# The place of the mixing matmuls in a step of the first scan: behind the first stream's convolution, or behind the second's

## What is computed

```python
x = x + _L0_conv_ref(_gn(x), centers, spreads, bias)   # token mixing, 4 heads
x = x + _L1_conv_ref(_gn(x), W)                        # a scan over the 64 rows

# _L0: einsum('mns,bwnvs->bwmvs', posmap, xr), posmap a softmax of 128x128 for each of 4 heads, plus a bias
# _L1, every image by itself:
def step(carry, row):
    new = row + relu(conv1d_same(carry, W))            # 9 taps over the tokens, 64 -> 64 channels
    return (new, new)
```

## Time and profile before

| what | value |
|---|---|
| median of 3 runs | 891.21 us (890.06 to 892.18) |
| the profiled execution | 893.26 us |
| its span | 891.3 us |
| busy in the span | PE 86%, PEld 81%, DVE 67%, ACT 53%, POOL 48% |
| granted TensorE clock, mean | 0.966 |
| first scan, first convolution of step 1 to last output transpose | 199.68 to 615.35 us |
| second scan, from its step 1 | 625.46 to 891 us |

### The profile page before, as it was taken

How to read it: one execution, slowest core, us unless ns; L and a number is a source line. 1 busy time by engine, 2 the same in 40 slices (tenths; PEclk the granted TensorE clock), 3 DMA queues, 4 the chain that set the end, 5 groups by cost and what they waited for, 6 DMA issues and landing times.

```text
span 891.3 us, 17386 instructions
## 1 busy us (share of the span) xinstructions
PE 764.4 (86%) x5546; PEld 718.1 (81%) x5546; DVE 595.3 (67%) x1265; ACT 476.8 (53%) x918; POOL 431.1 (48%) x416
## 2 busy tenths in 40 slices
PE   1677777769889898988989898997999999999997
PEld 1555556558888788887988887887999999999997
DVE  6699999955657567575776757555555555555553
ACT  1255555565456455555555555456555555555552
POOL 1677777725446445554454555453333333333332
PEclk9999998889999999999999999999899999999999
DMA  9755454023243243343333331111223222232323
GB/s 189 140 110 117 99 116 95 16 57 83 60 95 84 60 89 88 67 90 84 71 82 87 84 71 43 38 41 42 49 61 68 62 65 65 62 68 59 71 59 71
DMA packets 203149, 68.11 MB, mean 76 GB/s; under 512 B 137556, under 2 KB 203092, under 8 KB 203092
## 3 DMA queue, kind: packets, MB, share of 16 engines
q1 hardware_dynamic: 203092, 67.43, 34.8%
HBM read 33.85 MB, written 33.55 MB: 76 GB/s over the span
## 4 chain that ended last, share of the span: by engine, by line
PE 60%; DVE 17%; POOL 13%; issue 6%; ACT 2%; DVEq 0%; POOLq 0%; ACTq 0%
PE ps_conv L976 29%; PE ps_conv L980 14%; POOL xs L352 11%; PE ps_mix L892 9%; PE ps_out L968 4%; DVE st L668 3%; DVE st L550 3%; DVE carry L758 2%; DVE dev L613 2%; POOL total L379 2%; PE ps_in L905 2%; PE ps_small L882 1%; ACT x_paired L438 1%; DVE dev L618 1%; DVE x_sb L661 1%
## 5 line engine op out<-in xcount | busy, mean ns | idle before, releaser
L379 POOL TENSOR_TENSOR total<-x_paired,carry 128x256 f32<-128x256 f32 x256 | 188.3, 736 | 366.4 <-DVE carry L758 347.7
L480 ACT ACTIVATE carry_h<-carry 128x256 fp32r<-128x256 f32 x252 | 105.6, 419 | 298.3 <-DVE carry L758 298.3
L766 DVE TENSOR_TENSOR carry_l<-carry,carry_h 128x256 fp32r<-128x256 f32 x252 | 174.0, 690 | 90.6 <-ACT carry_h L480 90.6
L976 PE MATMUL ps_conv<-carry_h,wh 128*128 128x256 f32 x1280 | 221.7, 304 | 4.3 <-ACT carry_h L480 4.3
L758 DVE SCALAR_TENSOR_TENSOR carry<-ps_conv,rows 128x256 f32<-128x256 f32 x256 | 108.1, 422 | 163.4 <-PE ps_conv L980 158.5
L352 POOL TENSOR_TENSOR xs<-x_sb,rstd 128x512 f32<-128x512 f32 x104 | 193.5, 1886 | 39.5 <-DVE rstd L643 33.7
L438 ACT ACTIVATE x_paired<-ps_in,shift 64x512 f32<-64x512 f32 (+1 forms) x256 | 174.5, 682 | 68.4 <-PE ps_in L905 65.0
L976 PE MATMUL ps_conv<-carry_h,wl 128*128 128x256 f32 x1280 | 199.0, 286 | 0.0
L980 PE MATMUL ps_conv<-carry_l,wh 128*128 128x256 f32 x1280 | 198.9, 287 | 0.0
L976 PEld LDWEIGHTS ps_conv<-carry_h,wh 128*128 128x128 f32 x1280 | 180.2, 192 | 8.2 <-ACT carry_h L480 4.8
L976 PEld LDWEIGHTS ps_conv<-carry_h,wl 128*128 128x128 f32 x1280 | 175.0, 192 | 0.0
(11 more groups left out here) (92 smaller groups left out, 406.1 us busy)
## 6 DMA issues: line engine op xcount, KB each, us to landing
out_dram<-staged SPq DMA_DIRECT2D x256, 128.0 KB, 2.4
x_sb<-in_x_dram SPq DMA_DIRECT2D x52, 512.0 KB, 4.1
rows<-in_x_dram SPq DMA_DIRECT2D x12, 512.0 KB, 4.0
x_paired<-in_L_conv_W_dram SPq DMA_DIRECT2D x2, 80.0 KB, 2.9
x_paired<-in_L_conv_W_dram SPq DMA_DIRECT2D x2, 64.0 KB, 2.6
x_paired<-v_attention_centers_dram SPq DMA_DIRECT2D x1, 0.0 KB
x_paired<-v_attention_spreads_dram SPq DMA_DIRECT2D x1, 0.0 KB
bias_col<-v_token_proj_n_bias_dram SPq DMA_DIRECT2D x1, 0.5 KB, 5.7
```

The source lines that it names most:

```text
L379: nc.gpsimd.tensor_tensor(total[s][:, :].rearrange("p (w j) -> p w j", w=WS), x1_rows(wave, it, i, 1, s * WS, WS)[:, 0, :, :], carry[s][:, ...
L766: nc.vector.tensor_tensor(carry_l[s][:, :, EDGE:EDGE + J], carry[s][:, :].rearrange("p (w j) -> p w j", w=WS), carry_h[s][:, :, EDGE:EDGE ...
L976: nc.tensor.matmul(ps_conv[:, s * BANK:s * BANK + SW], w[:, d, :], carry_h[s][:, :, d:d + J], start=(w is wh and d == 0), stop=False)
```

## The change

In PE's `prep` the call of `mix_half` moves from the branch `after == 0` to the start of the branch `after == 1`. Nothing else differs. No instruction is added or removed on any engine, and the lists of DVE, ACT, POOL and SP are the same.

```diff
                         if prev:
                             pe.wait_ge(var2_ready, b)
                         mean1_of(b + 1, inv_p[:, :], 1)
+                else:
                     mix_half(b, i // 2, i % 2, ps_mix, b * CH + i // 2)
-                else:
                     if i == 0 and prev:
                         turn_in(b - 1, 1 - e, CH - 1)
                         shift1_of(b)
```

## The result

| | before | after |
|---|---|---|
| median of 4 runs each | 890.63 us (887.91 to 892.18) | 834.09 us (832.51 to 836.50) |
| ratio | | 0.936 (95%: 0.9343 to 0.9377) |
| profiled execution | 893.26 us | 832.51 us |
| window of the first scan | 199.68 to 615.35: 415.67 us | 197.25 to 554.60: 357.35 us |
| behind the window, to the end of the span | 275.95 us | 275.90 us |

The kernel is 6.4% faster. The two profiled executions lie 60.8 us apart. 58.3 of that is the first scan. 2.4 stand ahead of it, where no instruction has moved; other runs of these kernels and their variants begin the scan anywhere from 197.8 to 200.6 us, so I do not count it to the change. The medians differ by 56.5: the profiled execution of before was slower than its median and that of after faster.

A forecast was written before the change was run, and what follows sets the result against it. The prediction took a 6.30 us loop through POOL's `xs` to bound the first scan. Gains 48.9 + 0.8 + 2.1 less 3.6 gave 48.2, so 843 us on the median's basis; range 829 to 860, forecast's own 829 to 852.

The forecast's parts named there:

- What bounds the kernel: First scan: loop of second convolution, carry, `total`, `xs`, mixing takes 6.30 us a step, whatever else PE does.
- Gain: 48.9: Mixing pairs in the first scan: their whole wait for POOL's `xs`, 48.9 us, goes.
- From E of step i-1 ... `xs` is out at E + 3.58.: E: PE has issued the second stream's convolution; PE reaches the moved pair at 4.94 or 5.81 us, after `xs`.
- PE's list: Only PE's instruction order changes; no queue is passed on POOL, SP, ACT or DVE, and no DMA moves.
- What PE alone would need.: First scan window: PE's own work is 346.0 us of the 415.7 taken.
- I take 0.7: Step 6's small matmul: DVE 0.7 us later, waits of 0.74 and 2.3, together 9.9 against 10.7; gain 0.8.
- The clock ... I take half.: Half-speed stretches behind the long waits in blocks 8, 9 and 14: between 0 and 4.3 us back, gain 2.1.
- What is late next.: DVE lateness: 1.3 us at the loop's turn, 2.0 in other steps, 0.3 at the stage's end; loss 3.6.
- that I leave where they are: First scan window: 5.8 us beyond PE's own work, the named waits and the low clock, left unexplained.
- (a): Rival, chance 0.20: DVE bounds odd steps 3, 5 and 7 at 5.5 us rather than 4.94; 12 us, 855 us.
- (b): Rival, chance 0.03: POOL's `xs` holds up DVE's carry low part every step, 11.7 us a block; no change, 891 us.
- (c): Rival, chance 0.03: the `xs` wait returns at the pair's new place; slower, 930 us if `xs` is 3.2 us later.

The follow-up runs named there:

- even-steps kernel: Only the mixing pairs of even steps moved behind the second convolution, odd ones left in place, against the kernel before: 856.08 us against 892.96.
- odd-steps: Only the mixing pairs of odd steps moved behind the second convolution, even ones left in place, against the kernel before: 856.04 us against 892.96.
- behind-everything: The changed kernel with the mixing pair moved behind `turn_in` and the small matmuls, as the last thing of the step: 841.92 us.
- late-`xs` kernel: The changed kernel with POOL making `xs` in the step that uses it, behind the first `total`: 913.41 us against 891.67 for the kernel before.

## Why the prediction was right, and where it missed

The forecast was 843 us, faster with 0.94; it was faster, at 834.09. That lies inside the range of 829 to 860, near its fast end. The mechanism held and several sizes were off. By its steps:

- **What bounds the kernel, and "Gain: 48.9".** The wait for `xs` went from 48.9 us to none. That the loop was its cause is shown from both sides: shortening it on POOL took most of that wait away without touching PE's place for the pair, and closing it again at the new place made 81.4 us of wait.
- **"From E of step i-1 ... `xs` is out at E + 3.58."** Right in its conclusion, wrong as a constant. Where DVE is late, behind `mix_to_x1` for one, `xs` is late with it: out at E + 3.2 to 4.3 in the changed kernel and at up to E + 5.1 in the even-steps kernel. At the new place there is room for the former, at 4.94 and more. The forecast for the even-steps kernel rested on the constant and missed by 20 us.
- **"PE's list" and `x1_done`.** The prediction said of `mix_to_x1` only that it would meet no new wait. That the pair's second semaphore was itself nearly late at the old place went unseen, because a wait is put down to whoever comes last. Had the change been made on POOL instead, that would have been 18.8 us of error; for this change it cost nothing, since the move steps past both (at the new place `mix_to_x1` has ended 1.1 us or more before PE is there). For that the forecast had no argument: it is luck.
- **"What PE alone would need."** 346.0 us, and 44.1 for a block. The block measured 44.13 to 44.17 in two kernels.
- **"I take 0.7" for DVE's lateness at the small matmul.** This term was mis-sized. The matmul started at E + 2.00 in block 10 (324.30 - 322.30) where it had been E + 1.76, so 0.24 late, and at E + 3.45 in block 9 (279.90 - 276.45) where it had been E + 3.31, so 0.14. The carry ahead of it came at E + 0.56 in block 10 (322.86) in place of E + 0.31, the same quarter of a microsecond. The waits are 5.9 us in all against the 9.9 forecast: 4.0 more gained. The bound with no lateness, 5.0, was nearly the truth.
- **"The clock ... I take half."** All three stretches went, 2.2 more than forecast. Behind the 1.68 us wait of block 9 the granted clock stayed at 1.00, where it had been 0.62 behind the 2.41. The waits were not 2.3 but 1.7, by the mistake above; whether 2.3 would have brought the clock down is not shown.
- **"What is late next."** The loop's turn cost 1.6, with 1.3 forecast. "For other steps where DVE comes late, 2.0" did not happen: beside the small matmul, the loop's turn and the scan's two ends PE's weight loads have no row of waiting. That is 2.0 more gained, less 0.3.
- **The 5.8 us "that I leave where they are", and 0.3 for the end.** 357.35 - 346.0 - 5.9 - 1.6 leaves 3.9, so 2.2 of the 6.1 went too. The rows place most of it. The scan's first step runs in part at the lower clock in both kernels (windows below). From its first convolution to the `turn_out` of the step behind it is 8.25 us before and 9.47 after, where 1.83 + 0.43 + 0.85 + 2 x 1.83 = 6.77 is the full speed: 1.5 and 2.7 over, so here after is 1.2 worse. The last `turn_out` waited 1.34 us for `total` before and 0.47 after, 0.9 better. The three half-speed stretches of before, counted to the next `turn_out` but one, cost 4.7 rather than 4.3, and the 0.3 did not come. What is left, some 1.8 us, lay in before as 0.02 to 0.05 us at each pair that had waited.

The first step's window in before, with the granted clock as the third number from the end:

```profile
199.68:207.93 8.25, 8.25 (x53) 8.15 (x54) 3.81 (x8) 3.76 (x8) 2.76 (x5) 0.79 0.19 42
```

The same in after:

```profile
197.25:206.72 9.47, 9.47 (x53) 9.36 (x53) 4.26 (x8) 3.75 (x8) 3.86 (x5) 0.67 0.28 64
```

Together 4.0 + 2.2 + 1.7 + 2.2 = 10.1 us. That is the whole difference between the forecast window, 415.67 - 48.2 = 367.5, and the measured 357.35. The medians show a little less of it, 843 against 834.09, as the profiled execution of after was 1.58 below its own median and that of before 2.6 above.

The rivals: (a) would have shown itself in carries that no longer wait for PE, and they wait 47.5 us; blocks take 44.4, not the 46.5 that it needed (44.8, and 12 us over seven blocks). (b) asked for a middle duration of the low part over 1 us; it is 0.61. The mechanism behind (b) is real all the same, but strikes once a block, in step 6: in the looped blocks on a low part, which are the durations over 2 us of the earlier trace rows and cost PE nothing, in the others on the `dev` rows, where it costs 1.45 us. It is also why the waits of blocks 8, 9 and 14 are longer. (c) did not occur in the changed kernel. Made by hand it was slower, at 913 us; its rule (the wait counts, at either place, by how far `xs` comes behind the moment PE gets there) stood the test.

## What to carry to other kernels

When an engine waits once a step, draw the loop that leads back to it and divide its length by the number of steps it spans; moving the waiting instruction past one piece of independent work can make that number two, and was worth the whole wait here. Before that, look for a second semaphore at the same instruction and for how late the other engines become when the idle time is gone: a wait shows only its last releaser. Price what remains from the engine's own work in a block plus the waits that are left, and then take these away one by one.

## What the runs showed of the hardware

**Order of starts between VectorE and GpSimd.** A VectorE operation that starts while a GpSimd one runs can last until that one ends: 0.72 us in place of 0.19 under `total`, 1.65 in place of 0.62 under `xs`, with 128x32 elements only. Started 0.04 us ahead of `total`, it did not stretch. A tenth of a microsecond on another engine changed the kernel by 5 us. The Trainium skill, "SBUF — State Buffer", section "SBUF: two separate sides", has the rule: a VectorE operation with two inputs in SBUF and a GpSimd one that reads SBUF want the same port pair, and whoever starts first keeps it for the whole instruction. The two blocks above agree with it where VectorE comes second. That GpSimd is held when it comes second they do not show: `total` took 0.74 us with the `dev` row 0.04 ahead of it, and 0.73 without.

**The hardware loop.** POOL's `total` starts 0.1 us later behind its carry inside its loop than in written-out code (0.58 against 0.48), and DVE stands for 2.0 to 3.4 us at its loop's turn in the eleven traces whose DVE has the loop, put down to "issue". In the two kernels with that loop written out the stop is gone.

**The clock.** Over all kernels PE stood 12 times for 2.4 us or more in the blocks of the first scan. Behind seven of them the granted clock was 0.50 to 0.66 over the next microseconds, so for the most part at the lower of its two levels, 1.2 GHz in place of 2.4 (all three in the kernel before, one each in the even-steps, odd-steps and behind-everything kernels, and the 3.44 us stop of the late-`xs` kernel), behind five it stayed at 1.00, though the stops were as long. The 2.41 us stop of the earlier trace rows, in the kernel before, had 0.62 behind it, and this one of the odd-steps kernel, just as long, had 1.00:

```profile
287.45 0.30 PEld L882 LDWEIGHTS ps_small<-dev,inv_p 128*128 128x128 f32 x2 [2.41 <-DVE dev L618]
```

In the kernels with no stop over 2.0 us the clock did not fall behind the scan's first step at all; in the even-steps kernel it fell once behind a shorter one of 1.70, which had two others, of 1.07 and 0.51, just ahead of it. What tells the two outcomes apart is open.
